# A perceiver kernel: the last attention's input projections of three tiles as fp16 halves

## The chip, the cores and the metric

One core of a Trainium2 chip runs the whole program. The metric is the time on the device in microseconds, the median of several runs. Five engines work side by side, each through its own list of instructions in order: TensorE (PE: matmuls and transposes into PSUM), VectorE (DVE), ScalarE (ACT), GpSimd (POOL) and SyncE (SP, here only the issuer of DMAs). They meet at semaphores: `e.wait_ge(s(name), n)` holds everything that stands behind it in that engine's list.

## The reference

Two layers over x (2 x 256 rows of 256) with a context of 2 x 4096 rows; each layer is a cross attention, a self attention and a feed-forward part. The stages that matter here are the last two: a low-rank attention with 16 heads, and `_L1_ffn_ref`, which begins with a small attention over the axis of length 2:

```python
xq = jnp.einsum('btd,hrd->bthr', x, Q); xk = jnp.einsum('bud,hrd->buhr', x, K)
attn = jax.nn.softmax(scores / sqrt(dim), axis=3)
x = x + jnp.einsum('bthu,bud,hde->bte', attn, x, VO)        # low-rank attention
...
qkv = LN(x) @ in_proj_w.T + in_proj_b                       # (512 x 256) @ (256 x 768)
y1 = LN(x_ + mha(qkv) @ out_proj_w.T + out_proj_b)          # then a mixture of 8 experts
```

## The kernel before, in words

The 512 rows are four tiles of 128 rows. The low-rank attention (`low_rank_attention`, one function on each engine) is a software pipeline of 32 steps i (16 heads, two batches; each step is one half of a batch's work for two heads) and some steps to drain it. In step i

- PE forms the scores of steps i and i+1 when i is even (L760, 12 fp16 matmuls), transposes the probabilities of i-2 (`turn5`, L772, four fp32 transposes), multiplies those of i-3 with the values (`mix5`, L787, 12 fp16 matmuls of 256 columns) and adds the output projection of i-4 (`out5`, L803, 12 of the same).
- DVE takes the maximum of i (`max5`, L1649), normalizes i-1 (`norm5`, L1660 and L1662), forms the low fp16 half of the transposed probabilities of i-2 (`lo5`, L1654) and of the mixed rows of i-3 (`oT_lo`, L1710). `mix5(k)` waits for `lo5(k)`, `out5(k)` for `oT_lo(k)`, and `turn5(k)` for `norm5(k)`; the scores of step i wait for the exponentials of i-1.
- ACT forms the high halves (`hi5` L1202, `oT` L1208) and the exponentials (`exp5`, L1195).

The fp16 halves are how this kernel multiplies fp32 numbers at fp16 speed: a value is split into a high half and the rest, and three products (high x high, high x low, low x high) are summed.

Tiles 0 to 2 are complete before the pipeline ends, and their share of the last attention is put between its steps. Each engine has a generator of such early steps (`enter_last` on PE and DVE, `leave_pair` on ACT), and `LAST_AT` says at which half step (2i or 2i+1) each next one is taken. On PE 2i is ahead of `mix5`, 2i+1 behind `out5`; on DVE 2i is ahead of `lo5`, 2i+1 behind `oT_lo`; on ACT both are at the end of step i. The early steps before:

- DVE: three casts and `leave` (L1669: low-rank result added to X), norm statistics, the normalized rows (L1406), a copy of their transpose to SBUF (`latents`, L1676), then the bias added to each of six projection pieces (`project_early`, L1683), scores (`scores6`, L1742 on) and values (`values6`, L1751 to L1761) of the pair of tiles 0 and 2.
- PE: transpose of tiles 0 and 1 (L842), projection pieces n = 0 to 3 (L873, fp32, of 512 and 256 columns in turn, two chunks each), transpose of tile 2, pieces 4 and 5, then the turn of the attention's output (L834) and its projection (L853). All six pieces use PSUM bank 6, so piece n waits for DVE's addition of piece n-1 (`m_qkv0`).
- POOL: the reciprocal roots (L1295), biases (L1350, L1351), and after the sixth addition the products of queries and keys (`queries_times_keys`, L364), on which DVE's `scores6` waits (`m_prod`).

Tile 3 follows behind the loop in fp32 (L885, L887), then the rest of the last attention and the experts.

Of the kernel before, what the change touches and what calls it, by code (L numbers as in the profile page):

```python
# [19 lines left out]
ALU = mybir.AluOpType  # L20
# [3 lines left out]
F16 = mybir.dt.float16  # L24
U32 = mybir.dt.uint32

P = 128
# [39 lines left out]
LA_WAIT = 4  # L67
FILL = (18, 6, 30, 0, 30)
LAST_AT = (
    (49, 50, 51, 54, 55, 58, 59, 62, 70, 71,),  # L70
    (65, 70,),
    (43, 47, 48, 48, 50, 52, 54, 55, 55, 56, 57, 60, 62, 64, 67, 69,),
)
Y0_AT = 2

# [130 lines left out]
def build(nc, x, ctx, consts, cols, w_x, w_a, w_ao, b_a, w_f1, w_f2, w_f3, w_f4, w_g1, w_g2, w_g3, w_y, w_yv, b_yv,  # L206
          w_l, w_vo, w_in, w_out, rows6, w_gate, w_e1, b_e1, w_e2, b_e2, consts6, out):
    with ExitStack() as stack:
# [112 lines left out]
        b2r = wts[:, 2816:3840].rearrange("p (g n) -> p g n", g=E6 // 2)  # L321
        wgt = wts[:, 3840:3856].rearrange("p (c n) -> p c n", c=DC)
        b1c = wts[:, 3856:3920].rearrange("p (e f) -> p e f", e=E6)
        x0 = tail[:, 0:1024].rearrange("p (t d) -> p t d", t=NT)
        x0T = tail[:, 1024:2048].rearrange("p (c n) -> p c n", c=DC)
        o6 = tail[:, 2048:3072].rearrange("p (t d) -> p t d", t=NT)
# [43 lines left out]
        def _(sp):  # L370
# [42 lines left out]
            for j in range(4):  # L413
                sp.dma_start(wl_stage[:, 2 * j:2 * j + 2], w_l[:, 2 * j:2 * j + 2].rearrange("p j c n -> p j (c n)"))\
                    .then_inc(s("wl_in%d" % j), 16)
            load_w1 = lambda e: sp.dma_start(w1[:, e], w_e1[e].rearrange("(c p) f -> p c f", p=P)).then_inc(s("w1_in%d" % e), 16)
            load_w2 = lambda e: sp.dma_start(w2[e], w_e2[e].rearrange("(f p) d -> p f d", p=P)).then_inc(s("w2_in%d" % e), 16)
            def load_vo(q):

# [13 lines left out]
                load_vo(q)  # L433
            sp.wait_ge(s("vo_hi"), H5)
            sp.wait_ge(s("vo_lo"), H5)
            for dst, src in ((w6i, w_in), (w6o, w_out), (wgt, w_gate), (b1c, b_e1)):
                sp.dma_start(dst, src).then_inc(s("w6_in"), 16)
            for e in range(E6):
                sp.dma_start(b2r[64 * (e % 2):64 * (e % 2) + 64, e // 2, :], b_e2[e].partition_broadcast(64)).then_inc(s("w6_in"), 16)
# [25 lines left out]
        def _(pe):  # L465
# [392 lines left out]
            def enter_last():  # L858

                turn_latents(0, (0, 1), 6)  # L860
                yield
                pe.wait_ge(s("w6_in"), 16 * 14)
                for n in range(6):
                    t, cols = n // 2, ((0, 512), (512, 768))[n % 2]
                    if n == 4:
                        turn_latents(1, (2,), 6)
                        yield
                    if n in (0, 4):
                        pe.wait_ge(s("m_xT"), n // 4 + 1)
                    else:  # L870
                        pe.wait_ge(s("m_qkv0"), n)
                    for c in range(DC):
                        mm = pe.matmul(ps[:, 6, 0:cols[1] - cols[0]], x0T[:, c, t * P:(t + 1) * P], w6i[:, c, cols[0]:cols[1]],  # L873
                                       start=(c == 0), stop=(c == DC - 1))
                    mm.then_inc(s("m_qkv0_ps"), 1)
                    yield
                yield from leave_pair(0, 6, 6)
# [30 lines left out]
            def experts():  # L908
# [31 lines left out]
                def hidden(g):  # L940

                    if g == 0:
                        pe.wait_ge(s("m_dis"), 2)
                    else:
                        pe.wait_ge(s("m_h"), 2 * g)
                    pair = (2 * g, 2 * g + 1)
                    for e in pair:
                        pe.wait_ge(s("w1_in%d" % e), 16)
                    for f in range(2):
                        for c in range(DC):  # L950
                            for e in pair:
                                o = 64 * (e % 2)
                                mm = pe.matmul(ps[o:o + 64, f, :], disT[:, c, e * CAP:(e + 1) * CAP],  # L953
                                               w1[:, e, c, f * 512:(f + 1) * 512], start=(c == 0), stop=(c == DC - 1))
                    mm.then_inc(s("m_h_ps"), 1)
# [69 lines left out]
        def _(act):  # L1025
# [144 lines left out]
            def low_rank_attention():  # L1170
                def vo_hi(h):

                    act.wait_ge(s("x_in%d" % (h // 2 % 2)), 16 * (h // 4 + 2))
                    act.activation(vo_stage[:, h % 4], vo_stage[:, h % 4], ACT.Copy, scale=VO_SCALE).then_inc(s("vo_scaled"), 1)
                    act.wait_ge(s("vo_scaled"), h + 1)
                    act.activation(vo[:, h, 0], vo_stage[:, h % 4], ACT.Copy).then_inc(s("vo_hi"), 1)

                act.wait_ge(s("av"), 2 * NJ)
                def projected(n):
                    b, j = n // (H5 // 2), n % (H5 // 2)  # L1180
                    act.wait_ge(s("l_proj"), n + 1)
                    act.activation(QK5[:, 0, j, :, b * SEQ:(b + 1) * SEQ], bank(projection_bank(n), a=2), ACT.Copy).then_inc(s("l_hi"), 1)

                for n in range(H5 // 2):
                    projected(n)
                    if n == 2:
                        x_hi(1)
                        xT_hi(1)

                def exp5(i):  # L1190
                    act.wait_ge(s("l_max"), 2 * i + 2)
                    if i >= 2:
                        act.wait_ge(s("l_pt"), i - 1)
                    for t in range(2):
                        act.activation(P5[:, i % 2, t, :], ps[:, i % 2, t * SEQ:(t + 1) * SEQ], ACT.Exp, bias=nb5[:, i % 2, t:t + 1],  # L1195
                                       scale=1.0 / 16, accum_out=l5[:, i % 2, t:t + 1]).then_inc(s("l_exp"), 1)

                def hi5(i):
                    act.wait_ge(s("l_pt"), i + 1)
                    if i >= 2:  # L1200
                        act.wait_ge(s("l_pv"), i - 1)
                    act.activation(pth[:, i % 2, :], ps[:, 2 + i % 2, :], ACT.Copy).then_inc(s("l_pt_hi"), 1)  # L1202

                def oT(i):
                    act.wait_ge(s("l_pv"), i + 1)
                    if i >= 2:
                        act.wait_ge(s("l_vo"), i - 1)
                    act.activation(oT5[:, i % 2, 0], bank(4 + i % 2, a=DC), ACT.Copy).then_inc(s("l_ot_hi"), 1)  # L1208

                early = leave_pair(0, 6)  # L1210
                for n in late(-1):
                    projected(n)
                for i in range(2 * H5 + 4):
                    if 0 <= i - 2 < 2 * H5:
                        hi5(i - 2)
                    if i < 2 * H5:
                        exp5(i)
                    for n in late(i):
                        projected(n)
                    if 0 <= i - 3 < 2 * H5:  # L1220
                        oT(i - 3)
                    if i < H5:
                        vo_hi(i)
                    for _ in range(LAST_AT[ACTE].count(2 * i) + LAST_AT[ACTE].count(2 * i + 1)):
                        next(early, None)

            def leave_pair(j, b_turn):
                act.wait_ge(s("m_sub"), j + 1)
# [61 lines left out]
        def _(pool):  # L1290
# [54 lines left out]
            def biases(k, tiles):  # L1345

                w = [P, tiles.stop - tiles.start, D]
                pool.wait_ge(s("w6_in"), 16 * 14)
                pool.wait_ge(s("xn_turned"), NORM["m", k] + 1)
                pool.tensor_tensor(x0[:, tiles, :], x0[:, tiles, :], b6o.unsqueeze(1).broadcast_to(w), ALU.add).then_inc(s("x_bo"), 1)  # L1350
                pool.tensor_tensor(X[:, tiles, :], X[:, tiles, :], ln2b.unsqueeze(1).broadcast_to(w), ALU.add).then_inc(s("x_beta"), 1)  # L1351
# [16 lines left out]
        def _(dve):  # L1368
# [257 lines left out]
            def low_rank_attention():  # L1626
# [44 lines left out]
                def latents(k, tiles, n):  # L1671
                    yield from layernorm("m", k, x0[:, tiles[0]:tiles[-1] + 1, :], tiles)
                    yield
                    dve.wait_ge(s("xn_turned"), NORM["m", k] + 1)
                    w = len(tiles) * P
                    dve.tensor_copy(x0T[:, :, tiles[0] * P:tiles[0] * P + w], ps[:, n, 0:2 * w].rearrange("p (c n) -> p c n", c=DC))\  # L1676
                        .then_inc(s("m_xT"), 1)

# [5 lines left out]
                        yield  # L1684

                def enter_last():
                    dve.tensor_copy(ones16, ones[:, :])
                    dve.tensor_copy(tris16, tris)
                    dve.tensor_copy(id16, ident).then_inc(s("id16"), 1)
                    leave(0, slice(0, 2), H5)  # L1690
                    yield
                    yield from latents(0, (0, 1), 6)
                    yield
                    dve.wait_ge(s("w6_in"), 16 * 14)
                    yield from project_early(range(4))
                    leave(1, slice(0, 1), H5 + 8)
                    yield from latents(1, (2,), 6)
                    yield
                    yield from project_early((4, 5))
                    dve.wait_ge(s("m_prod"), 1)  # L1700
                    scores6(0)
                    yield
                    values6(0)
                    yield
# [268 lines left out]
```

## Time and profile before

| | us |
|---|---|
| median of 3 runs (lowest, highest) | 564.72 (564.54, 565.95) |
| the profiled execution's own time | 564.27 |
| its span in the trace | 562.4 |
| PE busy in the span | 516.6 (92%) |
| DVE busy | 353.7 (63%) |
| ACT busy | 283.3 (50%) |
| POOL busy | 76.6 (14%) |

Times in the trace run from the start of the span. A matmul's record is longer than its slot, since the next one starts before it ends; what a matmul costs in a stream is the distance of the starts, or the chain's row divided by its count. An fp32 matmul has two records.

### The profile page before, as it was taken

To read this page: it belongs to the slowest core of one execution; us is meant where nothing else is said; L and a number is where in the kernel's file an instruction comes from. 1 tells how busy PE (TensorE), PEld (TensorE's weight loads), DVE (VectorE), ACT (ScalarE), POOL (GpSimd) and SP (SyncE) were. 2 spreads that over 40 slices of the span, in tenths; PEclk is the share of its full clock that TensorE was granted. 3 is DMA by queue.
4 is the path that set the end of the run, shared out by engine and by line. 5 is a ranking of instruction groups with operands and counts; after the bars stand their busy time and mean duration, and the time that the engine had idled before them with its cause. 6 is when DMAs were issued, how large, how long until landed. Compare 5 with 4: busy or idle time off the path is not lost.

```text
span 562.4 us, 9402 instructions
## 1 busy us (share of the span) xinstructions
PE 516.6 (92%) x3556; PEld 356.1 (63%) x3556; DVE 353.7 (63%) x848; ACT 283.3 (50%) x616; POOL 76.6 (14%) x66
## 2 busy tenths in 40 slices
PE   7799998998999998999989998899999999888992
PEld 6565664565666654557545776788887788664551
DVE  4874646964448863265565666698878687744235
ACT  3777952537741038494267836888754453011110
POOL 0134131200012100000001401233201011200001
PEclk9999999999999999999999999999999999979997
DMA  8964580000000010000510040222282006950001
GB/s 275 314 200 91 114 183 5 1 2 1 1 1 0 1 29 1 1 1 0 176 50 1 2 150 1 76 77 76 84 327 101 1 1 212 350 187 1 1 0 38
DMA packets 45197, 44.06 MB, mean 78 GB/s; under 512 B 18656, under 2 KB 41184, under 8 KB 45024
## 3 DMA queue, kind: packets, MB, share of 16 engines
q1 hardware_dynamic: 45152, 43.45, 25.3%
q8 instruction: 29, 0.48, 0.3%
q14 instruction: 16, 0.13, 0.1%
HBM read 38.73 MB, written 0.52 MB: 70 GB/s over the span
## 4 chain that ended last, share of the span: by engine, by line
PE 65%; DVE 17%; issue 10%; ACT 6%; POOL 1%; DMA 1%; SPq 0%; DVEq 0%; ACTq 0%; POOLq 0%
PE ps L648 10%; PE ps L677 8%; PE ps L787 7%; PE ps L803 7%; PE ps L662 4%; PE ps L679 4%; PE ps L772 3%; PE ps L953 3%; PE ps L978 2%; PE ps L709 2%; PE ps L760 2%; PE ps L873 1%; DVE mx L1540 1%; ACT arena L1131 1%; ACT arena L1116 1%
## 5 line engine op out<-in xcount | busy, mean ns | idle before, releaser
L648 PE MATMUL ps<-ctx_tr,qtl 128*128 128x512 f16 x384 | 90.7, 379 | 2.1 <-ACT arena L1131 1.4
L1540 DVE TENSOR_REDUCE mx<-arena 128x1 f32<-128x512 f32 x64 | 43.1, 682 | 35.3 <-ACT arena L1131 34.7
L648 PEld LDWEIGHTS ps<-ctx_tr,qtl 128*128 128x128 f16 x384 | 36.7, 98 | 40.8 <-issue 3.2
L1131 ACT ACTIVATE arena<-ps 128x512 f32<-128x512 f32 x64 | 37.9, 596 | 43.9 <-PE ps L648 43.8
L677 PE MATMUL ps<-ctx_nat,pth 128*128 128x512 f16 x172 | 58.4, 379 | 0.0
L1116 ACT ACTIVATE arena<-arena,small 128x512 f32<-128x512 f32 x64 | 45.8, 716 | 6.3 <-DVE small L1549 6.2
L803 PE MATMUL ps<-arena,ctx_tr 128*128 128x256 f16 x384 | 47.2, 273 | 0.1
L679 PE MATMUL ps<-ctx_nat,ptl 128*128 128x256 f16 x172 | 46.9, 273 | 0.0
L662 PE MATMUL ps<-const,arena 128*128 128x128 f32 x256 | 39.1, 275 | 5.8 <-ACT arena L1116 5.1
L1295 POOL TENSOR_TENSOR rstd<-mv,col 128x2 f32<-128x2 f32 x13 | 9.9, 765 | 246.1 <-DVE mv L1400 245.9
L1554 DVE TENSOR_TENSOR ptl<-ps,pth 128x512 f16<-128x512 f32 x43 | 29.6, 688 | 21.6 <-ACT pth L1124 21.4
L662 PEld LDWEIGHTS ps<-const,arena 128*128 128x128 f32 x256 | 29.8, 140 | 17.8 <-ACT arena L1116 10.9
L803 PEld LDWEIGHTS ps<-arena,ctx_tr 128*128 128x128 f16 x384 | 37.5, 98 | 4.6 <-DVE ctx_tr L1710 0.3
L1202 ACT ACTIVATE pth<-ps 128x512 f16<-128x512 f32 x32 | 19.0, 594 | 33.2 <-PE ps L772 33.2
L1195 ACT ACTIVATE ctx_tr<-ps,small 128x256 f32<-128x256 f32 x64 | 29.6, 471 | 5.7 <-DVE work L1649 5.7
L470 PE MATMUL ps<-ones 128*128 128x256 f16 x244 | 31.5, 289 | 1.1 <-DVE ones L1888 1.1
L1124 ACT ACTIVATE pth<-ps 128x512 f16<-128x512 f32 x43 | 25.4, 591 | 9.0 <-PE ps L662 8.8
L470 PEld LDWEIGHTS ps<-ones 128*128 128x128 f16 x244 | 25.2, 104 | 6.4 <-DVE ones L1888 1.1
L677 PE MATMUL ps<-ctx_nat,arena 128*128 128x512 f16 x84 | 28.7, 379 | 0.0
L1649 DVE TENSOR_SCALAR_CACHE_REDUCE work<-ps 128x256 f16<-128x256 f32 x64 | 24.4, 418 | 6.3 <-PE ps L760 6.3
L1554 DVE TENSOR_TENSOR arena<-ps,arena 128x512 f16<-128x512 f32 x21 | 14.5, 690 | 20.9 <-ACT arena L1124 20.8
L677 PEld LDWEIGHTS ps<-ctx_nat,pth 128*128 128x128 f16 x172 | 16.8, 98 | 17.0 <-issue 1.4
(294 smaller groups left out, 1039.1 us busy)
## 6 DMA issues: line engine op xcount, KB each, us to landing
ctx_nat<-in_w_e SPq DMA_DIRECT2D x8, 1024.0 KB, 8.1
ctx_tr<-in_w_e SPq DMA_DIRECT2D x6, 1024.0 KB, 11.5
work<-in_ctx SPq DMA_DIRECT2D x8, 512.0 KB, 4.9
ctx_tr<-in_ctx SPq DMA_DIRECT2D x8, 512.0 KB, 7.2
work<-in_w_vo SPq DMA_DIRECT2D x8, 512.0 KB, 3.8
ctx_nat<-in_w_l SPq DMA_DIRECT2D x4, 512.0 KB, 5.4
arena<-in_w_e SPq DMA_DIRECT2D x2, 1024.0 KB, 7.3
wts<-in_rows SPq DMA_DIRECT2D x1, 1024.0 KB, 14.6
```

What stands on the lines that cost most here:

```text
L470: pe.matmul(ps[:, to, 0:SEQ], o[:, 0:P], o, start=True, stop=True, skip_group_check=True)
L648: mm = pe.matmul(ps[:, n % 2, :], qtl[:, qh, d, u * P:(u + 1) * P], CT[:, t0:t0 + KT, kh, d, :], start=(i == 0 and d == 0), stop=(i == 2 a ...
L662: mm = pe.transpose(ps[:, 4 + j % 2, i * P:(i + 1) * P], S[:, (j) % SRING, i * P:(i + 1) * P], ident)
L677: pe.matmul(ps[:, acc, :], PH[j % PRING][:, i * P:(i + 1) * P], CN[:, t].rearrange("p h d -> p (h d)"), start=(c == 0 and i == 0), stop=Fa ...
L679: mm = pe.matmul(ps[:, acc, 0:D], PL[j % PRING][:, i * P:(i + 1) * P], CN[:, t, 0, :], start=False, stop=(c == NCH - 1 and i == KT - 1), s ...
L787: mm = pe.matmul(ps[:, 4 + i % 2, d * SEQ:(d + 1) * SEQ], xl5[b][:, xh, u, d * P:(d + 1) * P], pt[:, i % 2, pu], start=(n == 0), stop=(n = ...
L803: mm = pe.matmul(ps[:, 6 + b, t * D:(t + 1) * D], oT5[:, i % 2, oh, c, p * P:(p + 1) * P], vo[:, h, vh, c, :], start=(i % H5 == 0 and p == ...
L1116: act.activation(S[:, j % SRING, :], S[:, j % SRING, :], ACT.Exp, bias=ebias[:, u:u + 1], scale=SCALES[L], accum_out=ls[:, u, c:c + 1]).th ...
L1131: act.activation(S[:, n % SRING, :], ps[:, n % 2, :], ACT.Copy).then_inc(s("score_copied"), 1)
L1195: act.activation(P5[:, i % 2, t, :], ps[:, i % 2, t * SEQ:(t + 1) * SEQ], ACT.Exp, bias=nb5[:, i % 2, t:t + 1], scale=1.0 / 16, accum_out= ...
L1540: dve.tensor_reduce(mx[:, u, c:c + 1], S[:, n % SRING, :], AX.X, ALU.max).then_inc(s("score_max"), 1)
L1554: dve.tensor_tensor(PL[j % PRING], ps[:, 4 + j % 2, :], PH[j % PRING], ALU.subtract).then_inc(s("pt_lo"), 1)
```

## The change

The six early projection pieces are computed as fp16 halves: three fp16 matmuls for each chunk in the place of one fp32 matmul. The weights `w6i` (128 x 1536) are split on the chip, the high half on ACT and the rest on DVE; the transposed rows of tiles 0 to 2 leave PSUM as halves too, the high one by ACT and the low one by DVE, in the place of DVE's copy. `LAST_AT` is written anew: ACT takes five early steps where it took two, DVE 17 where it took 16, and several stand elsewhere. `w6i` gets a semaphore of its own, and the two loads of a pair of experts share one (so that DVE, PE and POOL wait for 13 loads on `w6_in`, not 14).

```diff
 LAST_AT = (
-    (49, 50, 51, 54, 55, 58, 59, 62, 70, 71,),
-    (65, 70,),
-    (43, 47, 48, 48, 50, 52, 54, 55, 55, 56, 57, 60, 62, 64, 67, 69,),
+    (49, 51, 53, 54, 55, 58, 59, 62, 69, 71,),
+    (41, 49, 57, 67, 70,),
+    (42, 44, 46, 48, 49, 51, 52, 54, 55, 55, 56, 57, 60, 64, 65, 67, 69,),
 )
+        w6h = ctx_tr[:, 10752:12288].bitcast(F16).rearrange("p (h c n) -> p h c n", h=2, c=DC)
+        x6h = wts[:, 2048:2816].bitcast(F16).rearrange("p (h c n) -> p h c n", h=2, c=DC)
...
+            sp.dma_start(w6i, w_in).then_inc(s("w6i_in"), 16)
...
 # PE, enter_last
+                    pe.wait_ge(s("w6_lo"), 1)
                     for c in range(DC):
-                        mm = pe.matmul(ps[:, 6, 0:cols[1] - cols[0]], x0T[:, c, t * P:(t + 1) * P], w6i[:, c, cols[0]:cols[1]],
-                                       start=(c == 0), stop=(c == DC - 1))
+                        for k, (xh, wh) in enumerate(((0, 0), (0, 1), (1, 0))):
+                            mm = pe.matmul(ps[:, 6, 0:cols[1] - cols[0]], x6h[:, xh, c, t * P:(t + 1) * P],
+                                           w6h[:, wh, c, cols[0]:cols[1]], start=(c == 0 and k == 0), stop=(c == DC - 1 and k == 2))
...
 # ACT
-                early = leave_pair(0, 6)
+                early = enter_last()
+            def enter_last():
+                def latents_hi(k, tiles, n):
+                    act.wait_ge(s("xn_turned"), NORM["m", k] + 1)
+                    w = len(tiles) * P
+                    act.activation(x6h[:, 0, :, tiles[0] * P:tiles[0] * P + w], ps[:, n, 0:2 * w].rearrange("p (c n) -> p c n", c=DC),
+                                   ACT.Copy).then_inc(s("m_x_hi"), 1)
+                act.wait_ge(s("w6i_in"), 16)
+                act.activation(w6h[:, 0], w6i, ACT.Copy).then_inc(s("w6_hi"), 1)
+                yield
+                latents_hi(0, (0, 1), 6)
+                yield
+                latents_hi(1, (2,), 6)
+                yield
+                yield from leave_pair(0, 6)
...
 # DVE
                 def latents(k, tiles, n):
...
+                    if k < 2:
+                        dve.wait_ge(s("m_x_hi"), k + 1)
+                        dve.tensor_tensor(x6h[:, 1, :, tiles[0] * P:tiles[0] * P + w], ps[:, n, 0:2 * w].rearrange("p (c n) -> p c n", c=DC),
+                                          x6h[:, 0, :, tiles[0] * P:tiles[0] * P + w], ALU.subtract).then_inc(s("m_xT"), 1)
+                        return
...
                 def enter_last():
+                    dve.wait_ge(s("w6_hi"), 1)
+                    dve.tensor_tensor(w6h[:, 1], w6i, w6h[:, 0], ALU.subtract).then_inc(s("w6_lo"), 1)
+                    yield
```

## Rows read from the trace of the kernel before

**Rows 1.** The page's part 1: busy us, share of the span, instructions.
```profile
PE 516.6 (92%) x3556; PEld 356.1 (63%) x3556; DVE 353.7 (63%) x848; ACT 283.3 (50%) x616; POOL 76.6 (14%) x66
```

**Rows 2.** Busy time by stretch: window, its length, then each engine (instructions), PE clock, DMA.
```profile
412.00:430.00 18.00, 18.00 (x179) 15.28 (x177) 15.40 (x52) 10.10 (x30) 0.00 (x0) 1.00 0.75 303
430.00:467.00 37.00, 36.56 (x299) 29.10 (x298) 28.46 (x94) 16.81 (x49) 7.64 (x7) 1.00 0.00 1
467.00:478.00 11.00, 10.87 (x96) 9.40 (x94) 8.00 (x17) 3.73 (x7) 0.00 (x0) 1.00 0.84 270
```

**Rows 3.** The chain that ended last, in order of time: start us, us, work.
```profile
434.55 1.96 PE ps L873 x4
436.51 1.31 PE ps L787 x12
...
439.13 0.87 PE ps L873 x4
...
456.85 1.72 PE ps L873 x4
...
462.97 0.86 PE ps L873 x4
```

**Rows 4.** PE's timeline (start us, us, work, idle before), the earlier attention's 512-column fp16 matmuls.
```profile
298.52 1.67 PE L648 MATMUL ps<-ctx_tr,qtl 128*128 128x512 f16 x7
```

**Rows 5.** PE's timeline: step 23's `mix5(20)`, and around the first projection piece.
```profile
426.49 0.38 PE L787 MATMUL ps<-pth,ctx_tr 128*128 128x256 f16 x2
...
433.52 0.60 PE L772 MATMUL ps<-const,ctx_tr 128*128 128x128 f32 x4
434.55 1.96 PE L873 MATMUL ps<-work,ctx_tr 128*128 128x512 f32 x4 [0.44 <-DVE ctx_tr L1676]
```

**Rows 6.** DVE's timeline, steps 21 to 24.
```profile
420.66 0.68 DVE L1654 TENSOR_TENSOR ptl<-ps,pth 128x512 f16<-128x512 f32 x1
...
422.31 0.22 DVE L1687 CAST work<-ones 128x128 f16<-128x128 f32 x1
...
423.43 0.42 DVE L1649 TENSOR_SCALAR_CACHE_REDUCE work<-ps 128x256 f16<-128x256 f32 x1
...
424.12 0.16 DVE L1660 RECIPROCAL small<-small 128x2 f32<-128x2 f32 x1
...
424.85 0.68 DVE L1654 TENSOR_TENSOR ptl<-ps,pth 128x512 f16<-128x512 f32 x1
...
433.72 0.69 DVE L1676 COPY ctx_tr<-ps 128x512 f32<-128x512 f32 x1 [1.10 <-PE ps L842]
434.32 0.68 DVE L1654 TENSOR_TENSOR ptl<-ps,pth 128x512 f16<-128x512 f32 x1
434.92 0.68 DVE L1710 TENSOR_TENSOR ctx_tr<-ps,ctx_tr 128x512 f16<-128x512 f32 x1
```

**Rows 7.** Groups by form, whole span: splits of 1024 columns from SBUF (busy us, mean ns).
```profile
L1104 ACT ACTIVATE ctx_nat<-work 128x1024 f16<-128x1024 f32 x8 | 8.4, 1049 | 3.8 <-DMA work<-in_ctx 3.8
L1529 DVE TENSOR_TENSOR ctx_nat<-work,ctx_nat 128x1024 f16<-128x1024 f32 x4 | 4.9, 1223 | 0.8 <-ACT ctx_nat L1104 0.7
```

**Rows 8.** Timelines of POOL, PE and DVE where the pipeline drains (steps 32 to 35).
```profile
464.50 2.35 POOL L364 TENSOR_TENSOR ctx_nat<-ctx_nat 128x1024 f32<-128x1024 f32 x1 [8.72 <-DVE ctx_nat L1683]
...
466.29 0.60 PE L772 MATMUL ps<-const,ctx_tr 128*128 128x128 f32 x4
...
467.18 1.21 DVE L1742 TENSOR_REDUCE work<-ctx_nat 128x16 f32<-128x1024 f32 x1
468.84 0.69 DVE L1654 TENSOR_TENSOR ptl<-ps,pth 128x512 f16<-128x512 f32 x1
...
472.54 0.16 DVE L1751 TENSOR_TENSOR work<-work 128x8 f32<-128x8 f32 x1
...
475.23 0.69 DVE L1710 TENSOR_TENSOR ctx_tr<-ps,ctx_tr 128x512 f16<-128x512 f32 x1
...
475.97 1.48 PE L803 MATMUL ps<-arena,ctx_tr 128*128 128x256 f16 x12
```

More of the change, by code:

```diff
@@ L415, in _ @@
                     .then_inc(s("wl_in%d" % j), 16)
-            load_w1 = lambda e: sp.dma_start(w1[:, e], w_e1[e].rearrange("(c p) f -> p c f", p=P)).then_inc(s("w1_in%d" % e), 16)
+            load_w1 = lambda e: sp.dma_start(w1[:, e], w_e1[e].rearrange("(c p) f -> p c f", p=P)).then_inc(s("w1_in%d" % (e // 2)), 16)
             load_w2 = lambda e: sp.dma_start(w2[e], w_e2[e].rearrange("(f p) d -> p f d", p=P)).then_inc(s("w2_in%d" % e), 16)
@@ L435, in _ @@
             sp.wait_ge(s("vo_lo"), H5)
-            for dst, src in ((w6i, w_in), (w6o, w_out), (wgt, w_gate), (b1c, b_e1)):
+            sp.dma_start(w6i, w_in).then_inc(s("w6i_in"), 16)
+            for dst, src in ((w6o, w_out), (wgt, w_gate), (b1c, b_e1)):
                 sp.dma_start(dst, src).then_inc(s("w6_in"), 16)
@@ L861, in enter_last @@
                 yield
-                pe.wait_ge(s("w6_in"), 16 * 14)
+                pe.wait_ge(s("w6_in"), 16 * 13)
                 for n in range(6):
@@ L946, in hidden @@
                     pair = (2 * g, 2 * g + 1)
-                    for e in pair:
-                        pe.wait_ge(s("w1_in%d" % e), 16)
+                    pe.wait_ge(s("w1_in%d" % g), 32)
                     for f in range(2):
@@ L1347, in biases @@
                 w = [P, tiles.stop - tiles.start, D]
-                pool.wait_ge(s("w6_in"), 16 * 14)
+                pool.wait_ge(s("w6_in"), 16 * 13)
                 pool.wait_ge(s("xn_turned"), NORM["m", k] + 1)
@@ L1673, in latents @@
                     yield
+                    w = len(tiles) * P
+                    if k < 2:
[3 more added lines that the diff above has]
+                        return
                     dve.wait_ge(s("xn_turned"), NORM["m", k] + 1)
-                    w = len(tiles) * P
                     dve.tensor_copy(x0T[:, :, tiles[0] * P:tiles[0] * P + w], ps[:, n, 0:2 * w].rearrange("p (c n) -> p c n", c=DC))\
@@ L1693, in enter_last @@
                     yield
-                    dve.wait_ge(s("w6_in"), 16 * 14)
+                    dve.wait_ge(s("w6_in"), 16 * 13)
                     yield from project_early(range(4))
```

## The prediction

> **What bounds the kernel now.** I read the page's busy shares first: PE is busy for 92% of the span, DVE for 63% [rows 1]. A share over the whole span doesn't say what a change in one stage is worth, so the stretches come next. In the part of the low-rank pipeline where the early steps lie, PE is busy for 36.56 of 37.00 us, DVE for 28.46, ACT for 16.81, at full clock and with no DMA traffic to speak of [rows 2]. The chain of waits agrees: from 434 to 464 it runs through PE alone, and all six early projection pieces are links of it [rows 3]. So a microsecond taken off PE in this stage comes off the kernel, as long as DVE delivers the low halves (`lo5`, `oT_lo`) in time. DVE has 8.5 us to spare over 37 us, but its list is in order and the pipeline has two buffers, so the spare time counts only step by step. That is where the change has to be walked through. At the end of the pipeline, where PE's last `out5(31)` starts at 475.97, right behind DVE's `oT_lo(31)` of 475.23 [rows 8], DVE is on the path.
>
> **PE's work, removed and added.** Removed: three fp32 pieces of 512 columns and three of 256. Their links in the chain are 1.96, 1.72 and 1.72 us, and 0.87, 0.87 and 0.86 us (the six; four are shown) [rows 3]. The first holds some 0.16 us of pipeline end that shows only since PE had been idle ahead of it; I take 1.80 for it. Sum 1.80 + 2 x 1.72 + 2 x 0.87 + 0.86 = 7.84, and some 0.27 us at the seams to the scores' matmuls, which stay. Three pieces end ahead of scores (n = 1, 3, 4), and there the chain's row is already without the seam; for n = 0, 2 and 5 it stays in part. I count 0.1 us for these. Added: six fp16 matmuls for each piece. Those of 256 columns cost 1.31 / 12 = 0.109 us each [rows 3]; those of 512 columns, from the starts of seven in a row, (1.67 - 0.38) / 6 = 0.215 us [rows 4] (0.38 being the record of one). That is 3 x 6 x 0.215 + 3 x 6 x 0.109 = 3.87 + 1.96 = 5.83. The matmul work falls by 7.84 - 5.83 = 2.0 us, with 0.1 either way.
>
> Here a rule of the Trainium skill stands against the row. TensorE: Matmul & The Clock Gate, section Back-to-back issue gap, gives two numbers for a stream of 512-column matmuls: about 216 ns for the isolated gap, and about 131 ns for a sustained stream with its weight loads. By the second the six pieces would cost 3 x 6 x 0.131 = 2.36 us where I have 3.87, and the time would be 1.5 us lower. The trace's 0.215 us agrees with the first and contradicts the second; its chance as a rival is below.
>
> **The idle time ahead of the first piece.** Before, PE ends `turn5(23)` at about 433.52 + 0.44 = 433.96 and starts piece 0 at 434.55, as DVE's copy of the transposed rows isn't there [rows 5]. DVE itself had stood 1.10 us for that transpose [rows 6]. With the new places PE runs `mix5(22)` and `out5(21)` ahead of piece 0 (51 for 50), 2.6 us of work that covers the longer way of the rows (transpose, ACT's high half, DVE's low half; each half at most 0.69 us, as the copy [rows 6]). I walk it: transposes end at 433.9, ACT at 434.7, DVE at 435.4, piece 0 is due at 437.0. Gain 434.55 - 433.96 less a 0.05 seam = 0.54 us.
>
> **The weight split.** ACT takes 1.05 us and DVE 1.22 us for 1024 columns [rows 7]; for 1536 at most 1.57 and 1.83, I take 1.47 and 1.75 since a part is fixed. ACT does it at the end of step 20 (w_in was issued at 403 and has long landed) and has room: PE holds ACT up there, not the reverse. `hi5(19)` is 0.2 us later, and hidden. DVE does it in step 21 ahead of `lo5(19)`, which moves from 420.66 to 422.4 [rows 6]; PE wants that at 423.4, so it is covered. But it doesn't recover: a DVE step is 0.69 + 0.73 us (max, norm: 423.43, 424.12, 424.85) and twice 0.60 (434.32 to 434.92) = 2.62 us [rows 6], against 3.05 to 3.5 us for PE. `oT_lo(18)` is at 423.0, `max5(22)` at 423.6, `norm5(21)` ends at 425.0. Then stand the casts and `leave` (moved from the end of step 21, 422.31 to 423.43, 1.12 us), so `lo5(20)` comes at 426.1 instead of 424.85 and is ready at 426.8. `mix5(20)` wants to start at 426.49 [rows 5]. PE loses 0.35 us. From there to step 24 each further deadline is met by 0.2 us or more. Bounds: without any cover 1.75 us, and 0 if the split is 0.35 us shorter than I take it or DVE's slack is a bit larger.
>
> **The new places in the middle.** The addition of piece 1 stands on DVE at 52, ahead of `lo5(24)`; on PE piece 1 is at 53, behind `out5(22)`. DVE comes there at 440.8 and stands until piece 1 is done at 443.1, 2.3 us, with `lo5(24)` and `oT_lo(23)` queued behind it. PE wants `lo5(24)` at 443.3. What saves it is that piece 2 is now ahead of `mix5(24)` on PE: PE waits only for DVE's addition of piece 1 (the bank), 0.22 us, and in piece 2's 1.3 us the low half arrives. Cost 0.22 us; if the cover fails, `lo5(24)` ready at 444.2 costs 0.9. Tile 2's halves (transpose at 58 on PE, DVE waits at 57) hold DVE for 0.6 us while PE works on `mix5(26)` and `out5(25)`: nothing. DVE's deadlines up to step 31 are met by 0.5 us or more. Up to step 32 the balance is 2.0 + 0.54 - 0.35 - 0.22 = 1.97 us: `turn5(30)` starts at 464.3 for 466.29 [rows 8].
>
> **The drain.** Before, piece 5 was added at 62 and POOL's product (464.50, 2.35 us) was ready when DVE began `scores6` at 467.18 [rows 8]. Now the addition is at 64 and `scores6` at 65 of the same step, with only `lo5(30)` and `oT_lo(29)` between them. On the new clock: addition 465.2 to 465.6, POOL 465.7 to 468.1, `scores6` 468.15 + 1.66 (467.18 to 468.84) = 469.8. `lo5(31)` follows and is ready at 470.55, when PE wants it at 470.45: 0.1 us. Then `oT_lo(30)`, then `values6` from 471.0 for 2.69 us (472.54 to 475.23) to 473.7, and only then `oT_lo(31)`, and `out5(31)` at 474.45. Before it was 475.97, so of the 1.97 us ahead 1.52 are left: the drain costs 0.45. If POOL's product took 2.0 us instead, 0.35 of that would come back. Each 0.1 us by which POOL is later costs 0.1. The turn of the attention's output at 69 for 70 stands between the same two pieces of PE's list and changes nothing.
>
> **Behind the loop** nothing is changed: tile 3 stays fp32 and its wait chain is the same one, moved earlier. The merged semaphores of the expert loads and the count of 13 move no DMA; the loads of w1 end long ahead of their use. The clock was full in this stage with 0.4 us of idle time in 37 [rows 2] and PE is as dense afterwards, so I count nothing for it. Of the ACT steps, two more handovers of 0.6 and 0.4 us stand where PE holds ACT up: nothing.
>
> **Sum.** 2.0 + 0.54 - 0.35 - 0.22 - 0.45 = 1.5 us. Against the profiled execution (564.27) that gives 562.7; that one lies 0.45 below the median of the runs shown, so by the median 564.72 - 1.5 = 563.2.
>
> **Rivals.**
> 1. The thin stalls aren't there: the splits are a little shorter, POOL takes 2.0 us, and the new order has been counted by me too pessimistically by some tenths. Then 2.0 to 2.5 us remain: 562.2 to 562.7. For it: three of my four losses are under 0.4 us, less than the error of a walk of twelve steps. Against: the order of the lists forces them as computed.
> 2. DVE takes over as the pace in parts: further `lo5` and `oT_lo` are late, since DVE gets 1.75 us more work and at least 3 us more of standing, and a large part of PE's gain becomes waiting. 563.8 to 564.7, no change that can be measured. For it: margins of 0.2 us in steps 23 and 24.
> 3. Slower: the addition of piece 1 stands ahead of `lo5(24)`, and the cover by piece 2 doesn't work (the pipeline's low halves stay late from then on). Then DVE's standing is paid by PE: 2.3 us there, and 0.4 and 0.6 us at the two low halves of the rows, 3.3 in place of 0.22. 564.72 - 1.5 + 3.1 = 566.3. It decides from 1.5 us of extra PE waiting. For it: an in-order DVE with two buffers; against: 0.4 to 0.9 us are regained in each following step, as DVE's 2.62 us stand against PE's 3.05 to 3.5.
> 4. The sustained rate of 131 ns holds for the new pieces: 561.7. In this trace 384 such matmuls show 0.215 us in a stream [rows 4], so hardly.
>
> **Chances.** Forecast as walked 0.55 (own range 562.6 to 563.8); rival 1 0.22; rival 2 0.13; rival 3 0.08; rival 4 0.02. A difference of 0.3%, 1.7 us, is about what can be told from no change here; the forecast of 1.5 us lies just inside it, and I give 0.20 of its 0.55 to the side beyond. Faster by over 0.3%: 0.20 + 0.22 + 0.02 = 0.44. Within: 0.35 + 0.13 = 0.48. Slower: 0.08. The range takes in rivals 1 and 2 and leaves out most of 3: 561.9 to 565.0.
>
> **What would show it.** In the profile after: fp16 pieces of 1.3 and 0.65 us in place of L873's; PE idle 0.3 us ahead of `mix5(20)`, 0.2 ahead of piece 2, none ahead of piece 0; DVE idle for over 2 us ahead of the addition of piece 1, and until POOL is done ahead of `scores6`; the start of `turn5(30)` 2.0 us earlier and that of `out5(31)` 1.5. Wrong would be PE waits of over 0.5 us at any `mix5` or `out5`, or a lead that shrinks behind step 32 by other than about 0.45 us.

## The result, and the profile after

| | before | after |
|---|---|---|
| median (lowest to highest, runs) | 564.67 (563.70 to 566.08, 22) | 563.70 (562.52 to 565.86, 22) |
| the profiled execution's own time, its span | 564.27, 562.4 | 562.52, 560.6 |

The ratio of after to before is 0.9981, with a 95% interval of 0.9973 to 0.9989: 1.1 us faster (0.6 to 1.5). A second measurement gave 563.18 for 564.48, ratio 0.9976 (0.9964 to 0.9988). The forecast was 563.2.

The profiled execution of after is the fastest of its 22, so the spans overstate the difference. A sharper measure is the pipeline itself, from the start of `scores5(20)`, the last point that neither kernel's early steps have touched, to the start of `out5(31)`, PE's last work of the pipeline [rows 8 have it for before, 475.97]. That start itself lies between 414.97 and 415.91 us in the 14 profiled executions, so 0.9 us of a span's end has nothing to do with the change.

In the changed kernel the lines have other numbers. PE: L763 scores, L775 `turn5`, L790 `mix5`, L806 `out5`, L845 the tiles' transposes, L878 the pieces, L856 the output's projection. DVE: L1713 the weights' low half, L1697 the rows' low half, L1674 `lo5`, L1738 `oT_lo`, L1708 the additions, L1770 `scores6`. ACT: L1199 `exp5`. POOL: L366 the products. First before, then after, PE's timeline (start us, us, work, idle before):

```profile
415.16 0.83 PE L760 MATMUL ps<-ctx_tr 64*128 64x256 f16 x12
```
```profile
415.29 0.83 PE L763 MATMUL ps<-ctx_tr 64*128 64x256 f16 x12
...
426.94 0.39 PE L790 MATMUL ps<-pth,ctx_tr 128*128 128x256 f16 x2 [0.16 <-DVE ptl L1674]
...
437.04 1.46 PE L878 MATMUL ps<-ctx_tr,wts 128*128 128x512 f16 x6
438.43 0.83 PE L763 MATMUL ps<-ctx_tr 64*128 64x256 f16 x12
...
442.95 0.60 PE L775 MATMUL ps<-const,ctx_tr 128*128 128x128 f32 x4
443.63 1.47 PE L878 MATMUL ps<-ctx_tr,wts 128*128 128x512 f16 x6
444.94 0.38 PE L790 MATMUL ps<-pth,ctx_tr 128*128 128x256 f16 x2
...
464.43 0.60 PE L775 MATMUL ps<-const,ctx_tr 128*128 128x128 f32 x4
...
474.47 1.49 PE L806 MATMUL ps<-arena,ctx_tr 128*128 128x256 f16 x12
```

Before: 475.97 - 415.16 = 60.81 us. After: 474.47 - 415.29 = 59.18 us. The pipeline gives 1.63 us, and it repeats: two further executions of these places had 59.18 again (e0, e9). A 512-column piece takes 444.94 - 443.63 = 1.31 us where L873 took 1.72 [rows 3]. Piece 0 at 437.04 has no idle time ahead of it (0.44 before [rows 5]). The two small waits are at `mix5(20)` (426.94) and at piece 2 (443.63, where 442.95 + 0.44 would have been possible).

DVE's and POOL's timelines of after, the places that the prediction walked through:

```profile
420.79 1.75 DVE L1713 TENSOR_TENSOR ctx_tr<-work,ctx_tr 128x1536 f16<-128x1536 f32 x1
...
426.19 0.69 DVE L1674 TENSOR_TENSOR ptl<-ps,pth 128x512 f16<-128x512 f32 x1
...
434.81 0.69 DVE L1697 TENSOR_TENSOR wts<-ps,wts 128x512 f16<-128x512 f32 x1 [0.32 <-ACT wts L1235]
...
443.15 0.42 DVE L1708 TENSOR_TENSOR ctx_nat<-ps,wts 128x256 f32<-128x256 f32 x1 [2.36 <-PE ps L878]
...
468.16 1.22 DVE L1770 TENSOR_REDUCE work<-ctx_nat 128x16 f32<-128x1024 f32 x1 [0.46 <-POOL ctx_nat L366]
...
473.72 0.69 DVE L1738 TENSOR_TENSOR ctx_tr<-ps,ctx_tr 128x512 f16<-128x512 f32 x1
```
```profile
465.78 2.35 POOL L366 TENSOR_TENSOR ctx_nat<-ctx_nat 128x1024 f32<-128x1024 f32 x1 [11.22 <-DVE ctx_nat L1708]
```

The reader is to see three things: the split of the weights took the 1.75 us taken for it; DVE stood 2.36 us for piece 1 (2.3 predicted); and `scores6` (L1770) now waits for POOL's product, which puts `oT_lo(31)` (473.72) 0.75 us ahead of `out5(31)`, on the path.

### The profile page after: what moved, and what is told of

The parts are those of the page before. It is cut to its first block, busy times and chain, and to the rows that moved or that the text cites. A ratio compares the mean times of both kernels' runs of the same rounds, so it can differ in the third digit from the quotient of the medians.

```text
span 560.6 us, 9435 instructions
## 1 busy us (share of the span) xinstructions
PE 514.9 (92%) x3568; PEld 355.5 (63%) x3568; DVE 355.2 (63%) x849; ACT 285.3 (51%) x619; POOL 76.6 (14%) x66
## 4 chain that ended last, share of the span: by engine, by line
PE 62%; DVE 19%; issue 10%; ACT 6%; POOL 1%; DMA 1%; SPq 0%; DVEq 0%; ACTq 0%; POOLq 0%
PE ps L651 10%; PE ps L680 8%; PE ps L790 6%; PE ps L806 6%; PE ps L665 4%; PE ps L682 4%; PE ps L957 3%; PE ps L982 3%; PE ps L775 2%; PE ps L712 2%; PE ps L763 1%; DVE mx L1560 1%; ACT arena L1135 1%; PE ps L878 1%; ACT arena L1120 1%
## 5 line engine op out<-in xcount | busy, mean ns | idle before, releaser
L806 PE MATMUL ps<-arena,ctx_tr 128*128 128x256 f16 x384 | 47.2, 273 | 0.1
L806 PEld LDWEIGHTS ps<-arena,ctx_tr 128*128 128x128 f16 x384 | 37.5, 98 | 4.6 <-DVE ctx_tr L1738 0.3
L1199 ACT ACTIVATE ctx_tr<-ps,small 128x256 f32<-128x256 f32 x64 | 29.7, 472 | 7.4 <-DVE work L1669 7.3
```

The source lines that it names most:

```text
L806: mm = pe.matmul(ps[:, 6 + b, t * D:(t + 1) * D], oT5[:, i % 2, oh, c, p * P:(p + 1) * P], vo[:, h, vh, c, :], start=(i % H5 == 0 and p == ...
```

## The experiments

Each was profiled once and timed beside the kernel before. Pipeline is the stretch defined above; the part behind it is from the start of `out5(31)` to the end of the span. Clock is the mean of the granted clock over the timed runs. In `LAST_AT` the three lists are PE's, ACT's and DVE's, as in the change, and the edits of `LAST_AT` are cut to their new lines. e1 and e8 are edits of the kernel before, the others of the changed kernel; the mended kernel of e6, e10 and e11 is that of e5. Where the split of the weights moves to 37 and 38 (e7, e5, e6, e10, e11), it stands ahead of the stretch's start; the distances of the scores up to there are 7.02 and 7.03 us in all these traces, so it doesn't move that start.

| run | pipeline us | behind it us | median us | ratio (95%) | clock |
|---|---|---|---|---|---|
| before (profiled once) | 60.81 | 86.43 | 564.5 to 564.7 | 1 | 0.9853 to 0.9865 |
| after, 22 runs | 59.18 | 86.13 | 563.70 | 0.9981 (0.9973, 0.9989) | 0.9844 |
| e0_after | 59.18 | 86.66 | 563.18 | 0.9976 (0.9964, 0.9988) | 0.9857 |
| e1_order_only | 60.84 | 86.36 | 564.44 | 1.0001 (0.9989, 1.0014) | 0.9861 |
| e2_pool_split | 60.33 | 86.18 | 563.85 | 0.9990 (0.9979, 1.0001) | 0.9862 |
| e3_mend_order | 58.77 | 86.84 | 562.89 | 0.9968 (0.9954, 0.9981) | 0.9858 |
| e4_old_places | 60.31 | 86.42 | 564.15 | 0.9987 (0.9975, 1.0000) | 0.9852 |
| e7_split_early | 58.86 | 87.01 | 563.14 | 0.9965 (0.9949, 0.9981) | 0.9863 |
| e5_best | 58.24 | 86.66 | 562.50 | 0.9958 (0.9943, 0.9974) | 0.9850 |
| e6_best_fill | 58.23 | 84.44 | 559.86 | 0.9920 (0.9895, 0.9946) | 0.9910 |
| e11_best_again | 58.24 | 86.75 | 562.38 | 0.9962 (0.9944, 0.9980) | 0.9862 |
| e8_before_fill | 60.82 | 86.72 | 564.82 | 1.0008 (0.9996, 1.0021) | 0.9862 |
| e9_after_fill | 59.18 | 84.67 | 561.64 | 0.9952 (0.9938, 0.9965) | 0.9888 |
| e10_fill_shift | 58.24 | 88.97 | 564.43 | 0.9994 (0.9983, 1.0005) | 0.9862 |

**After once more.** No edit.

> The changed kernel once more, as the measure for the other runs of this call. My theory: PE's last product group of the pipeline, out5(31), starts at 474.5 us of the span (475.97 before), a lead of 1.5 us, and the time is 1.0 to 1.5 us below the kernel before. Rival (the lead is given back behind the loop, where the clock falls to half for some microseconds): out5(31) still starts at 474.5, but from there to the end it takes longer than the 86.4 us of the kernel before.

The pipeline took 59.18 us. The part behind it was 86.66 us here and 86.13 in the first profile, with 86.43 before. Two executions of one kernel differ by 0.5 us there, so these can't tell whether some tenths of the lead are given back, as the rival says; all the runs together are looked at below.

**The order without the halves.**

```diff
 LAST_AT = (
+    (49, 51, 53, 54, 55, 58, 59, 62, 69, 71,),
+    (67, 70,),
+    (44, 46, 48, 49, 51, 52, 54, 55, 55, 56, 57, 60, 64, 65, 67, 69,),
```

> Only the new places of the early steps, on the arithmetic before: the six pieces stay fp32, nothing is split, DVE copies the transposed rows. My theory (the gain is PE's matmul work, 2.0 us, and 0.54 us of idle time ahead of piece 0; the new places cost 0.22 at piece 2 and 0.45 in the drain): 0.54 - 0.22 - 0.45, so out5(31) starts at 476.1, 0.1 us later than before, and the time is that of the kernel before within 0.3 us. Rival (the order brings the gain, the fp16 halves little): out5(31) at 474.9 or earlier, time 1.0 us lower.

60.84 us for 60.81, time unchanged. The rival is out: the new places alone bring nothing. What they gain ahead of piece 0 they lose at piece 2 and in the drain: by the starts of the scores, with piece 1's 0.87 us put aside as it moved, 0.67 us are gained between `scores5(24)` and `scores5(26)`, 0.34 lost between 26 and 28 and 0.36 from `scores5(30)` to `out5(31)`.

**The halves without the order.**

```diff
 LAST_AT = (
+    (49, 50, 51, 54, 55, 58, 59, 62, 70, 71,),
+    (41, 48, 57, 65, 70,),
+    (42, 43, 47, 48, 48, 50, 52, 54, 55, 55, 56, 57, 60, 62, 64, 67, 69,),
```

> The fp16 halves and the splits of the changed kernel, but the steps stand where they stood before (the weights' low half at 42, right ahead of the casts at 43). Measured from the start of scores5(20) to the start of out5(31): before 60.81 us, changed kernel 59.18. My theory: piece 0, ahead of mix5(22) again, now waits for transpose, ACT and DVE, 1.1 us of idle PE, while the drain loses nothing and piece 2 finds its bank free: 59.6 us, so the new places are worth 0.4 us and the halves by themselves 1.2. Rival (the places were only needed for room and bring nothing): 59.2 or less.

Here the split stands at 41 and 42, right ahead of the casts. 60.31 us, 0.7 longer than expected. PE's and DVE's timelines around piece 0:

```profile
433.71 0.66 PE L845 MATMUL ps<-const,ctx_tr 128*128 128x128 f32 x4 [0.32 <-DVE ctx_tr L1426]
434.20 0.60 PE L775 MATMUL ps<-const,ctx_tr 128*128 128x128 f32 x4
435.82 1.46 PE L878 MATMUL ps<-ctx_tr,wts 128*128 128x512 f16 x6 [1.02 <-issue]
```
```profile
435.03 0.69 DVE L1697 TENSOR_TENSOR wts<-ps,wts 128x512 f16<-128x512 f32 x1 [1.38 <-ACT wts L1235]
```

PE stands 0.32 us for the normalized rows and then over 1 us. The view names nothing for that second wait ("issue"), but the rows' low half (L1697) ends at 435.72, 0.10 us ahead of piece 0: it is the wait for the halves, which come by way of ACT and DVE. The walk had 1.1 us for the whole. So the halves alone are worth 60.81 - 60.31 = 0.50 us, the places alone 60.81 - 60.84 = -0.03, both together 1.63. They need each other: the longer way of the rows must be covered by `mix5(22)` and `out5(21)`. Both e4 and the changed kernel also pay the late `lo5(20)`.

**The weights' low half on POOL.**

```diff
 # DVE's split is taken out (and its place 42); POOL:
+            pool.wait_ge(s("w6_hi"), 1)
+            pool.tensor_tensor(w6h[:, 1], w6i, w6h[:, 0], ALU.subtract).then_inc(s("w6_lo"), 1)
             layernorm("m", 0)
```

> The changed kernel, but the low half of the weights (128x1536) is formed by POOL, idle from 403 to 430 us, in the place of DVE. My theory (DVE's 1.75 us make lo5(20) late and cost PE 0.35 us): the idle time of PE ahead of mix5(20) is gone and out5(31) starts 0.35 us earlier than in the changed kernel, at 474.1; POOL needs 3.2 us by its rate of 2.13 us for 1024 columns and is done by 423.5, long before piece 0. Time 0.3 to 0.4 us lower than the changed kernel. Rival (thin stalls aren't real, or POOL's reads hold DVE up): out5(31) at 474.5 or later.

The stretch became 1.15 us longer than in the changed kernel, not 0.35 shorter. DVE's and POOL's timelines:

```profile
420.56 3.44 DVE L1684 TENSOR_SCALAR ctx_tr<-ctx_tr,small 128x256 f32<-128x256 f32 x2
```
```profile
420.49 3.10 POOL L1374 TENSOR_TENSOR ctx_tr<-work,ctx_tr 128x1536 f16<-128x1536 f32 x1 [17.04 <-ACT ctx_tr L1239]
```

L1684 is `norm5`, two tensor_scalars from SBUF to SBUF in fp32, which take 0.62 us together elsewhere. Here they began 0.07 us behind POOL's subtraction and took 3.44 us; the first of them alone took 3.18. POOL was done at 423.59 and the pair at 424.00, and `lo5(19)` stood behind it. From `scores5(22)` to `scores5(24)` 8.50 us passed where it was 7.36, which is the 1.15. The Trainium skill (SBUF — State Buffer, section Who interferes with whom) says that a DVE copy or tensor_scalar in a two-port mode and a GpSimd instruction need the same port pair, and that the second one is fully blocked until the first ends. The times here agree; no row shows the mode in which these tensor_scalars ran.

The forecast of the run failed at the sentence that POOL's idle time is free; the second half of its rival came true. The trace of before had shown it, on the same pair (L1662 there) and a shorter POOL instruction:

```profile
371.26 1.16 POOL L1342 TENSOR_TENSOR arena<-work,arena 128x512 f16<-128x512 f32 x1 [3.23 <-ACT arena L1176]
371.52 1.31 DVE L1662 TENSOR_SCALAR ctx_tr<-ctx_tr,small 128x256 f32<-128x256 f32 x2
```

The pair ends at 372.83, 0.41 us behind POOL's 372.42, as in e2. In the trace of before it is so for all nine such pairs that begin over 0.2 us ahead of the end of a POOL instruction: they take 0.63 to 1.31 us and end 0.41 or 0.42 us behind it. The four that begin 0.15 or 0.16 us ahead of it take 0.61 or 0.62 us, as elsewhere.

**Three stalls mended by order.** PE's piece 1 at 52 for 53, DVE's casts and `leave` at 45 for 44, its last addition at 62 for 64.

```diff
+    (49, 51, 52, 54, 55, 58, 59, 62, 69, 71,),
     (41, 49, 57, 67, 70,),
+    (42, 45, 46, 48, 49, 51, 52, 54, 55, 55, 56, 57, 60, 62, 65, 67, 69,),
```

> The changed kernel with four steps at other places, each against one stall of the walk: DVE's casts and leave at 45 for 44 (behind oT_lo(19), so lo5(20) is in time: 0.35 us), PE's pieces 1 at 52 for 53 (so that DVE doesn't stand 2.3 us and piece 2 finds its bank free: 0.22 us), DVE's last addition at 62 for 64 (POOL's product is ready when scores6 comes: 0.42 us). My theory: out5(31) starts 1.0 us earlier than in the changed kernel, at 473.5, and the time is 0.9 to 1.0 us lower than its. Rival (DVE's total load is the bound): less than half of that comes.

0.41 us of the 1.0. Between the starts of the scores, piece 2's stall went (9.63 us for 9.88 from `scores5(26)` to `scores5(28)`), and the drain took 17.27 us for 17.62. The first repair moved its stall and made it larger: `leave` now delays `max5(23)` and so ACT's exponentials, `scores5(24)` comes only 0.05 us earlier, and the stretch from there to `scores5(26)` takes 9.00 us for 8.76, most of it since `lo5(21)` is late in turn.

```profile
429.42 0.83 PE L763 MATMUL ps<-ctx_tr 64*128 64x256 f16 x12 [0.21 <-ACT ctx_tr L1199]
```

**The split two steps earlier** (ACT at 37 for 41, DVE at 38 for 42), where DVE has slack of its own.

```diff
     (49, 51, 53, 54, 55, 58, 59, 62, 69, 71,),
+    (37, 49, 57, 67, 70,),
+    (38, 44, 46, 48, 49, 51, 52, 54, 55, 55, 56, 57, 60, 64, 65, 67, 69,),
```

> The changed kernel with the split of the weights two steps earlier (ACT at 37 for 41, DVE at 38 for 42), nothing else. My theory (lo5(20) was late since 1.75 us of split and 1.12 us of casts and leave stood within two steps, and DVE has only some 0.9 us of slack a step): PE's stall of 0.35 us ahead of mix5(20) goes, scores5(20) to out5(31) takes 58.85 us for 59.18. Rival (another thing makes lo5(20) late): 59.18.

58.86 us, as expected: the stall ahead of `mix5(20)` came from the split and the casts within two steps.

**All of them**, the split at 37 and 38, piece 1 at 52, the last addition at 62:

```diff
+    (49, 51, 52, 54, 55, 58, 59, 62, 69, 71,),
+    (37, 49, 57, 67, 70,),
+    (38, 44, 46, 48, 49, 51, 52, 54, 55, 55, 56, 57, 60, 62, 65, 67, 69,),
```

> The split two steps earlier, PE's piece 1 at 52 for 53, DVE's last addition at 62 for 64; casts and leave stay at 44. My theory: all three stalls go (0.35, 0.25, 0.35 us), scores5(20) to out5(31) 58.25 us, 0.93 less than the changed kernel and 2.56 less than before; time about 562.5 with 564.5 for the kernel before. Rival (as with the reordering that brought 0.41 for 1.0, each repair makes something else late): over 58.7 us.

58.24 us, 562.5 us in the median: 2.4 us below the kernel before by the ratio (1.5 to 3.2). The pipeline is 0.94 us shorter than the changed kernel's; in the medians that difference isn't clear of noise, as the intervals of the two ratios touch or overlap.

**The part behind the loop.** The changed kernel's granted clock was 0.9857 in the mean where the kernel before had 0.9865 beside it. So I filled the pauses of PE behind the loop, on the mended kernel first. `FILL` counts filling matmuls at five places there (fp16, 128 columns by 256, their result unused).

```diff
-FILL = (18, 6, 30, 0, 30)
+FILL = (18, 6, 43, 2, 34)
```

> The same, with more filling matmuls where PE is idle behind the loop (43 for 30, 2 for 0, 34 for 30). Theory (of two executions of one kernel the one with the lower mean granted clock is longer, and the changed kernel was given 0.9844 to 0.9857 where the kernel before had 0.9865, which is part of why less than the 1.6 us of the pipeline shows in the median): with fewer pauses the mean clock over the runs rises towards 0.99 and the time falls by 0.3 us or more against the kernel without the filling. Rival: the clock falls for another reason, or the filling stands in the way of the chain at the lower clock: mean clock the same, time the same or 0.3 us higher.

559.86 us, and the part behind the pipeline was 2.2 us shorter. Busy time and clock (the number behind POOL's) of the mended kernel, without and with filling:

```profile
486.00:506.00 20.00, 14.92 (x95) 11.56 (x93) 11.31 (x36) 3.27 (x7) 0.86 (x1) 0.83 0.59 203
```
```profile
486.00:506.00 20.00, 16.04 (x121) 11.95 (x119) 12.91 (x43) 3.27 (x7) 0.86 (x1) 1.00 0.56 193
```

Taken as a mean over the time, 0.83 is 6.8 of the 20 us at the lower level (1.2 GHz) and the rest at 2.4 GHz. The eight fp32 records of the output projection show it: 3.78 us without, 2.00 with.

```profile
492.56 3.78 PE L856 MATMUL ps<-work,ctx_tr 128*128 128x256 f32 x8 [0.69 <-ACT ctx_tr L1252]
```
```profile
491.52 2.00 PE L856 MATMUL ps<-work,ctx_tr 128*128 128x256 f32 x8 [0.69 <-ACT ctx_tr L1252]
```

**The same filling on before and after**, to see whether its worth adds:

> The kernel before, with only the filling matmuls behind the loop (43 for 30, 2 for 0, 34 for 30). Theory (the pauses of PE between 488 and 501 us are followed by stretches at half the clock, and the filling takes these away whatever the pipeline does): the part from out5(31) to the end takes 84.4 us for 86.4, and the time is about 2.2 us below the kernel before, at a mean clock near 0.99. Rival (the fall of the clock depends on where the pipeline ends): no change or under 1 us.

> The changed kernel with the same filling matmuls. Theory (the change is worth its 1.63 us of the pipeline, and the medians of 1.0 and 1.3 us differ from that by the clock stretches behind the loop, which vary between executions): with these stretches gone in both kernels the difference between this and the kernel before with filling comes out at 1.6 us, within 0.3. Rival (part of the 1.63 us is really given back behind the loop): the difference stays at 1.0 to 1.2 us.

It doesn't add. On the kernel before it is worth nothing (the clock of that stretch stays at 0.83), on the changed one 1.5 to 2.1 us by medians of different measurements. With filling the two kernels are 3.2 us apart (564.82 and 561.64), further than the pipeline's 1.63, so neither theory of these two runs is borne out. The 561.64 is a median of five, and the next run shows how little such a median holds.

**The same, 2.6 us later, and the best once more:**

```diff
-FILL = (18, 6, 43, 2, 34)
+FILL = (42, 6, 43, 2, 34)
```

> The mended kernel with filling, plus 24 filling matmuls (24 x 0.109 = 2.6 us) right behind the pipeline, so that all that follows stands 2.6 us later, where it stood in the kernel before. The filling alone gained 2.6 us on the mended kernel, 1.5 to 2 on the changed one and nothing on the kernel before. Theory (whether the clock falls at 490 to 500 us depends on where in time the short pauses of the last attention stand, not on their length alone): the time rises by more than the 2.6 us, by 4 to 5, with half clock between 486 and 506 us again. Rival (the filling and the mended order keep the clock up wherever they stand): it rises by 2.6 us and the clock stays full there.

> The mended kernel with filling once more, on this chip, beside the shifted one: 559.9 us as before if its gain of 4.8 us holds, and full clock from 486 to 506 us; 561.5 or more if that was a lucky set of executions.

Against e6 the shift took the part behind the pipeline from 84.44 to 88.97 us, 4.5 more for 2.6 us of filling, with the clock of 486 to 506 us at 0.83 again. But the repetition without shift gave 562.38, 0.83 and 86.75 us. A mean clock over 0.99, that of the execution with full clock there, was seen in four of six executions in the one measurement and in one of twelve in the other. Against this repetition, timed beside it, the shifted kernel is only 2.05 us slower and has the same clock in that stretch, so e10's theory isn't borne out: the filling costs about what it takes. And e6's 4.8 us don't hold up; what holds is 2 to 2.5 us, the same as without filling. The three measurements ran on three chips (e4 to e7 on one, e8 and e9 on another, e0 to e3, e10 and e11 on a third), and no run tests whether that matters for the clock.

## Why the prediction came out as it did

The forecast of 563.2 lies between the two medians, 563.70 and 563.18, and its mechanism was seen step by step. Relative to `scores5(20)` it had `out5(31)` at 474.45 - 415.16 = 59.29 us; measured 59.18. Its signs came as named, and no `mix5` or `out5` waited over 0.5 us, so rivals 1, 2 and 3 are out. So is rival 4: six pieces' matmuls take 1.31 us, 0.218 each. (Its 384 is the count of L648; the rate was read from seven of them.)

- **What bounds it.** Right. The medians follow the pipeline's stretch over eight kernels without filling, from 60.8 us (564.4 to 564.7) over 60.3 (563.9 to 564.2), 59.2 (563.2 to 563.7) and 58.8 to 58.9 (562.9 to 563.1) to 58.2 (562.5).
- **PE's work, 2.0 us.** Right: 512-column pieces at 1.31 us for a calculated 1.29 and a former 1.72; e4, with 0.50 us of it left, shows that this saving reaches the end only where nothing else waits. The terms close: 1.63 us measured, with 0.33, 0.24 and 0.36 us of losses put back and the 0.54 us ahead of piece 0 taken off, leaves 2.02 (1.89 with the 0.67 that e1 gained there).
- **The idle time ahead of piece 0, 0.54 us.** Piece 0 waits for nothing now; e1, with the order alone, gained 0.67 there. e4 adds what the prediction didn't price: in the old places the halves would have made this wait longer, to over 1 us.
- **`lo5(20)` late, 0.35 us.** Right: `scores5(24)` is 0.33 us later relative to `scores5(20)` (14.38 for 14.05 us), and e7 takes exactly that away.
- **The new places, 0.22 us.** Right: 0.24 us at piece 2, and e3 regains 0.25.
- **The drain, 0.45 us.** Right in cause, 0.1 us too large: relative to `scores5(20)`, `turn5(30)` is 1.99 us earlier (49.14 for 51.13; 1.97 forecast) and `out5(31)` 1.63, so the drain cost 0.36. e3 regains 0.35.
- **A thing that was missed** without harm: a DVE normalization that begins well within a POOL instruction ends only behind it. e2 shows that the order of such a pair can cost more than a microsecond, and the trace of before had it.
- **Behind the loop, 0 us.** This term is the one that the runs don't bear out. The pipeline gave 1.63 us and the medians show 0.97 and 1.30, and e3, e7 and e5 also show about 0.4 us less in the median than in the pipeline (1.60 for 2.04, 1.55 for 1.95, 2.19 for 2.57), while e4 and e2 (0.54 for 0.50, 0.63 for 0.48) show nothing less. In the profiled executions the part behind is 86.13 to 87.01 us, 86.66 in the mean, in after, e0, e3, e7 and e5, and 86.18 to 86.43, 86.35 in the mean, in before, e1, e2 and e4. Hardly one of these differences is clear of noise by itself (1.63 is within the interval of the second measurement, 0.7 to 2.0, and just outside that of the first); together they point at 0.3 to 0.4 us given back behind the loop. So the forecast's saving of 1.5 us was met by the pipeline and is more than the medians show. That 563.2 stands so near to 563.18 is in part luck, as the kernel before was at 564.48 in that measurement and not at the forecast's 564.72.
- **The clock as the reason** fits a part of this and isn't shown. Of the 22 executions of after seven were at a mean clock of 0.979 to 0.982 and took 563.8 to 565.9 us, where those at 0.988 and 0.989 took 562.5 to 563.3. Of the profiled kernels without filling, e3 and e7 have the longest part behind (86.84 and 87.01) and the lowest clock from 486 to 506 us (0.75 and 0.76, where before, after, e0 and e5 have 0.83 or 0.84). But by mean clock the change doesn't lower it: after was at 0.9844 and 0.9857, e7 at 0.9863, and the kernel before itself lay between 0.9853 and 0.9865 from one measurement to the next.

The chances were fair: 0.48 for a difference within 0.3% and 0.44 for more, with a measured 0.19% and 0.24%.

**Open.** What decides whether the clock falls around 490 to 500 us, and whether a shorter pipeline makes it fall for longer. It differs between executions of one kernel (e6, e11). Whether the time at which the last attention's pauses come matters isn't shown: e10 and e11 had the same clock there, and e8 and e9 differ in more than that time.

## What to carry to other kernels

When work on the bounding engine is exchanged for work that passes through two others first (here halves by ACT and DVE), the places of the steps are part of the price: halves and places were worth 0.50 and -0.03 us alone, and 1.63 together. In-order lists can be walked from measured starts: the prediction's losses came out to a tenth of a microsecond each, but the shorter walks of e3 and e4 missed by 0.6 and 0.7 us, as they stopped at the stall in question and left out what stood behind it. What a walk misses altogether is the sharing between engines that no semaphore shows; an instruction whose longest record is three times its usual one is the sign to look for (L1662 in before: 1.05 us for 0.35). An idle GpSimd isn't free while DVE normalizes fp32 rows in SBUF. And a saving of 1 us has to be read off a stretch of the trace, as executions of one kernel differ by twice that and more (562.5 to 565.9 us).

## What the runs showed of the hardware that wasn't expected

- A POOL subtraction of 3.10 us (128x1536, SBUF to SBUF) stretched two DVE tensor_scalars from 0.62 to 3.44 us, which started 0.07 us behind it. In before nine such pairs, begun over 0.2 us ahead of the end of a POOL tensor_tensor, ended 0.41 or 0.42 us behind it.
- The same filling of PE's pauses changed the time by +0.2, -1.5 to -2.1, and -0.1 to -2.6 us, depending on the kernel and on the measurement. In the execution with full clock, the eight fp32 records behind the pipeline took 2.00 us, where it had fallen 3.78.
